# A softmax over 16 groups of 64 scores: maxima subtracted and sums taken on DVE, one wide exponential on ACT

## What is computed

```python
scores = jnp.einsum('bhqd,bhkd->bhqk', Q, K) / jnp.sqrt(jnp.float32(D))   # 16 heads, D = 32
_, topi = jax.lax.top_k(scores, k)                                        # k = min(64, S) = S
attn = jax.nn.softmax(scores * sparse_mask, axis=-1)                      # the mask is all ones
out = jnp.einsum('bhqk,bhkd->bhqd', attn, V)
```

## Time and profile before

| | before |
|---|---|
| median of three runs | 1848.55 us (1845.55 to 1848.74) |
| profiled execution | 1843.91 us, of it 1842.1 us span from first to last instruction |
| instructions | 38062 |
| mean granted TensorE clock | 0.986 |
| PE / PEld busy | 1749.4 / 1505.1 us (95% / 82% of the span) |
| DVE / ACT / POOL busy | 966.4 / 834.2 / 182.4 us (52% / 45% / 10%) |
| cross, self, ff stage | about 0 to 846.7, 846.7 to 1354.0, 1354.0 to 1842.1 us |

### The profile page before, as it was taken

The page is one execution under the profiler, slowest core; times in us unless marked ns, Lnnn a source line. Parts: engine busy times, 40 slices in busy tenths (PEclk is TensorE's granted clock), DMA queues, the critical chain, the costliest instruction groups (busy, mean ns, idle before and its releaser), DMA issues.

```text
span 1842.1 us, 38062 instructions
## 1 busy us (share of the span) xinstructions
PE 1749.4 (95%) x15364; PEld 1505.1 (82%) x15364; DVE 966.4 (52%) x1506; ACT 834.2 (45%) x2793; POOL 182.4 (10%) x267
## 2 busy tenths in 40 slices
PE   5999999999999999959999999999879999999999
PEld 4888888888888888848888888888768888888887
DVE  4655555555555555553455555555654454445433
ACT  4555555555555555546754545454432222222221
POOL 1000000000000000001121212121030111011100
PEclk9999999999999999979999999999989999999999
DMA  4011111111111111133101001010200011101000
GB/s 184 1 47 47 48 47 47 48 47 48 47 47 47 47 37 37 70 120 154 48 25 40 28 32 36 23 46 23 76 35 17 30 46 47 41 5 46 23 24 23
DMA packets 39453, 86.60 MB, mean 47 GB/s; under 512 B 4768, under 2 KB 4896, under 8 KB 38048
## 3 DMA queue, kind: packets, MB, share of 16 engines
q1 hardware_dynamic: 39328, 84.77, 12.8%
HBM read 59.58 MB, written 25.17 MB: 46 GB/s over the span
## 4 chain that ended last, share of the span: by engine, by line
PE 81%; ACT 7%; DVE 4%; POOL 3%; issue 2%; DMA 2%; SPq 0%; POOLq 0%; DVEq 0%; ACTq 0%
PE project L316 40%; PE project L1498 13%; PE scores L556 6%; ACT self_probs L368 4%; PE scores L1512 3%; PE scores L1514 3%; PE probs_t_psum L1514 3%; PE probs_t_psum L1512 3%; PE probs_t_psum L566 3%; PE attended_t L583 2%; POOL self_residual L1447 1%; DMA x<-self_residual 1%; PE probs_t_psum L1098 1%; DVE row_max L358 1%; POOL rstd L932 1%
## 5 line engine op out<-in xcount | busy, mean ns | idle before, releaser
L1498 PE MATMUL project<-ff_xt,w_ternary 128*128 128x512 f32 x1024 | 255.9, 392 | 1.7 <-DVE ff_xt L988 1.7
L1547 ACT ACTIVATE hidden<-project,b_sb 128x512 f32<-128x512 f32 x128 | 88.3, 690 | 325.3 <-PE project L1498 324.1
L1498 PEld LDWEIGHTS project<-ff_xt,w_ternary 128*128 128x128 f32 x1024 | 190.1, 188 | 40.3 <-issue 1.9
L1572 DVE CAST hidden_hi<-hidden 128x512 fp32r<-128x512 f32 x128 | 56.8, 443 | 229.8 <-ACT hidden L1547 228.9
L368 ACT ACTIVATE self_probs<-scores,exp_bias 128x64 f32<-128x64 f32 x512 | 151.9, 350 | 55.5 <-DVE exp_bias L360 55.5
L316 PE MATMUL project<-self_xt_hi,self_w_hi 128*128 128x256 f32 x512 | 149.1, 291 | 2.4 <-DVE self_xt_lo L1299 2.3
L316 PE MATMUL project<-self_xt_hi,self_w_lo 128*128 128x256 f32 x512 | 146.0, 285 | 0.7 <-ACT self_probs_t L1235 0.7
L316 PE MATMUL project<-self_xt_lo,self_w_hi 128*128 128x256 f32 x512 | 146.0, 285 | 0.0
L368 ACT ACTIVATE cross_scores_probs<-cross_scores_probs,exp_bias 128x128 f32<-128x128 f32 x256 | 99.1, 394 | 88.0 <-DVE exp_bias L360 88.0
L929 POOL TENSOR_TENSOR var_eps<-mean_var,ln_eps 128x1 f32<-128x1 f32 x96 | 19.9, 208 | 1171.1 <-DVE mean_var L793 706.2
L556 PE MATMUL scores<-cross_k_t,q_pad 128*128 128x128 f32 x1024 | 127.0, 277 | 2.8 <-DVE cross_scores L827 1.3
(11 more groups left out here) (151 smaller groups left out, 4266.0 us busy)
## 6 DMA issues: line engine op xcount, KB each, us to landing
ctx_raw<-in_ctx SPq DMA_DIRECT2D x64, 256.0 KB, 3.8
cross_x<-in_x SPq DMA_DIRECT2D x32, 256.0 KB, 2.7
x<-cross_x SPq DMA_DIRECT2D x32, 256.0 KB, 2.1
self_x<-x SPq DMA_DIRECT2D x32, 256.0 KB, 2.8
ff_w_raw<-in_w SPq DMA_DIRECT2D x2, 4096.0 KB, 18.1
x<-self_residual SPq DMA_DIRECT2D x32, 256.0 KB, 2.1
ff_x<-x SPq DMA_DIRECT2D x32, 256.0 KB, 3.6
out<-ff_residual SPq DMA_DIRECT2D x32, 256.0 KB, 2.2
```

The lines of the kernel that those rows point to most:

```text
L1498: last = nc.tensor.matmul(PJ[m % 2][:], w1_q[:, c, cols], x_t[parity(v)][:, c, :], start=(c == 0 and x_t is fxt_hi), stop=(c == DC - 1 and ...
L1547: nc.scalar.activation(h_raw[:, m % 2, :], PJ[m % 2][:], ACT.Relu, bias=b1_sb[:, m:m + 1]).then_inc(h_relu, 1)
L1572: nc.vector.tensor_copy(h_hi[:, m % 4, :], h_raw[:, m % 2, :]).then_inc(h_hi_ready, 1)
```

## The change

In the self stage alone, DVE follows its reduction of the maxima with one subtraction: it writes the scores less their group's maximum, 128x1024, from PSUM into a new SBUF tile `self_scores_shifted` (the maxima as a broadcast operand). The multiplication that made a bias goes. ACT takes one exponential of the whole 128x1024 from that tile, with the scale and no bias and no accumulator. The sums are then taken by DVE, as a reduction over the exponentials at the start of `divide`, before the reciprocal. A semaphore `s_shifted` now says that PE may write the next scores, in place of `p_ready`; `p_sum` orders the sum before the reciprocal.

```diff
--- before.py
+++ after.py
@@ -216,6 +216,7 @@
             sat_hi = sb(st, "self_at_hi", [P, DC, P], F32R)
             sat_lo = sb(st, "self_at_lo", [P, DC, P], F32R)
             f_scratch = sb(st, "ff_weight_scratch", [P, 512])
+            s_d = sb(st, "self_scores_shifted", [P, 1024])
 
             s_stages = [sq_t[:].rearrange("p a c b s -> p (a c b s)"),
                         sk_t[:].rearrange("p a c b s -> p (a c b s)"),
@@ -267,7 +268,9 @@
                 self.s_free = s("s_free")
                 self.s_max = s("s_max")
                 self.s_bias = s("s_bias")
+                self.s_shifted = s("s_shifted")
                 self.p_ready = s("p_ready")
+                self.p_sum = s("p_sum")
                 self.p_scale = s("p_scale")
                 self.p_norm = s("p_norm")
                 self.pt_full = s("pt_full")
@@ -1078,7 +1081,7 @@
 
             def scores(u, t):
 
-                wait(e, G.p_ready, total(u, NT, t))
+                wait(e, G.s_shifted, total(u, NT, t))
 
                 for c in range(DC):
                     for b in range(2):
@@ -1226,7 +1229,9 @@
                 last.then_inc(G.pj_free[bank], 1)
 
             def exponentials(u, t):
-                exponentials_of(e, G, lambda k: total(u, NT, t + k), t, HEADS, S, s_p)
+                wait(e, G.s_shifted, total(u, NT, t + 1))
+                nc.scalar.activation(s_p[:], s_d[:], ACT.Exp, scale=SCORE_SCALE) \
+                    .then_inc(G.p_ready, 1)
 
             def probs_t_out(u, t):
                 wait(e, G.pt_full, total(u, NT, t + 1))
@@ -1327,11 +1332,19 @@
                                         ALU.add).then_inc(G.pj_free[bank], 1)
 
             def maxima(u, t):
+                rows = lambda a: a[:].rearrange("p (g k) -> p g k", g=HEADS)
                 wait(e, G.s_full, total(u, NT, t + 1))
-                row_bias(e, G, lambda k: total(u, NT, t + k), t, HEADS,
-                         S[:].rearrange("p (g k) -> p g k", g=HEADS))
+                nc.vector.reduce_max(row_max[:], rows(S), AXIS.X).then_inc(G.s_max, 1)
+                wait(e, G.s_max, total(u, NT, t + 1))
+                nc.vector.tensor_tensor(rows(s_d), rows(S),
+                                        row_max[:].unsqueeze(2).to_broadcast([P, HEADS, SEQ]),
+                                        ALU.subtract).then_inc(G.s_shifted, 1)
 
             def divide(u, t):
+                wait(e, G.p_ready, total(u, NT, t + 1))
+                nc.vector.reduce_sum(row_sum[:], s_p[:].rearrange("p (g k) -> p g k", g=HEADS), AXIS.X) \
+                    .then_inc(G.p_sum, 1)
+                wait(e, G.p_sum, total(u, NT, t + 1))
                 divide_by_sums(e, G, lambda k: total(u, NT, t + k), HEADS, s_p[:])
 
             def residual(u, t, kind):
```

## The result

| | before | after |
|---|---|---|
| median | 1847.05 us (1844.70 to 1848.74) | 1826.44 us (1825.19 to 1829.39) |
| profiled execution | 1843.91, span 1842.1 | 1829.39, span 1827.6 |
| DVE busy | 966.4 | 1044.0 |
| ACT busy | 834.2 | 715.5 |

A forecast was written before the change was run, and what follows sets the result against it. PE, busy 1749.4 of 1842.1 us, was taken as the bound, stalled by ACT's queue. Terms -20.1 - 1.7 + 1.2 + 0.7 = -19.9 us took the 1848.55 us median to 1828.6; range 1819 to 1839.

The forecast's parts named there:

- PE waited for ACT's queue: Self stage, units 0 to 13: the K drain sits behind sixteen exponentials on ACT; PE waits 16.5 us in 14 pieces.
- The prices: Per tile: wide exponential 1.05 us on ACT, subtraction 1.24 and sum 1.22 on DVE; 4.63 and 0.17 removed.
- The slacks: Steady unit, tile 1: 1.0 us spare before V's first projection matmul, 1.4 before the transposes, 1.4 before V's second.
- The loop: Units 0 to 13: 14 waits gone at 1.44 us each, 20.1 gained, plus 1.7 from unit 0's softmax waits.
- The 0.26 on each wait: PE in the self stage: each wait costs 0.26 us beyond its listed length, 1.51 against 1.25.
- Unit 14: Last but one self unit: DVE divides late, after two ternary weight chunks, so the sum adds 1.2 us.
- Unit 15: Last self unit: DVE divides late, after a DMA wait; the sum adds 1.22 us, nearly paid back, net 0.7 slower.
- The 4.63 us removed from ACT: Per tile on ACT: sixteen exponentials with accumulator reads, from first start to the next instruction, 4.63 us, go away.
- (c): Rival: nothing gained, because another chain, POOL's or a DMA, sets the unit's period; 1848 us, chance 0.05.
- (d): Rival: DVE's longer path in tile 1 takes over; at three times the price 29 us slower, 1878; chance 0.03.
- (e): Rival: the wide exponential costs what the sixteen did, so ACT is not shortened; 15 us slower, 1863; chance 0.03.
- (b): Rival: part of the K drain wait stays, through dearer subtraction or exponential or late POOL; half the gain, 1839; chance 0.07.

The follow-up runs named there:

- half of the change: The changed kernel with the subtraction kept on DVE, but sixteen exponentials with accumulators on ACT and no sum on DVE: 1847.03 us, ratio 1.0005.

## Why the prediction was right

- **PE waited for ACT's queue.** Shown from both sides: taking the drain out of that queue brings each steady unit to the same 30.01 us with the old softmax (1827.25; only the 2.0 us of unit 0 are missing); a shorter queue by another way, no bias, does too (1822.11); two more exponentials bring the wait back under its name.
- **The prices.** Subtraction 1.224 us (1.24 taken), exponential 1.060 (1.05), sum 1.209 (1.22).
- **The slacks.** For the transposes of tile 1 1.54 us were there (1.4 taken), for V0 1.41 (1.0). On DVE one more sum was free and a second not, and two more exponentials on ACT were too many.
- **The loop.** Units 0 to 13 lost 3.38 + 1.36 + 1.41 + 11 x 1.49 = 22.5 us in the first pair of profiles and 23.8 in the second profile of the changed kernel; 20.1 + 1.7 = 21.8 were summed. The 0.26 on each wait was about right: 1.49 a unit for a listed 1.18, and the two added waits cost 0.21 and 0.24 us more than listed.
- **Unit 14.** The wait went from 2.39 to 3.64, 1.25 for the 1.2 forecast. The sum stands on DVE between the second chunk and the reciprocal:

```profile
1281.52 1.21 DVE L1345 TENSOR_REDUCE row_sum<-self_probs 128x16 f32<-128x1024 f32 x1
...
1283.05 1.22 DVE L383 TENSOR_TENSOR self_probs<-self_probs,row_scale 128x1024 f32<-128x1024 f32 x1
```

  The unit grew by 1.22 in one profile and by 2.39 in the other, where the lower clock lasted longer.
- **Unit 15.** The mis-sized term: 0.7 forecast, 0.9 until the transposes, and 1.73 or 4.05 for the whole unit. I had allowed 1 to 2 us for the clock; kernels with the old form differ there by 3.5 us among themselves, so most of it is the execution, not the change. I had also read the granted clock of 0.72 from a stretch that I called the end of the last unit; it is its first 30.22 us, and the unit went on to 1360.27. In the first pair of profiles the start, the clock and the tail hide about a third of the gain: 1.48 (start) - 22.5 + 2.39 + 4.05 + 0.1 = -14.5 us, where the medians say -20.6 and -22.3.
- **Luck.** The sum of -19.9 came within 1 us of the measured -20.6 partly because two misses have opposite signs: in the second profile the loop gave 2.0 us more than summed and the tail cost 2.95, not 1.9. The range would have held either alone.
- **The 4.63 us removed from ACT.** 1.48 of them were the price of the bias operand, which the prediction never named; it did not matter to its sum, since all sixteen instructions went.
- **Rivals.** (c) falls with PE busy 360.44 of 361.31 us. (d) needed 2.84 us more of DVE work on that path than the change brought; by the measured slack and gain it is 1.54 + 1.49 = 3.0, not reached by the change nor by the two spare sums. (e) falls with 1.06 us for the wide exponential. (b) did not occur, and the two more exponentials show what it would have looked like: 1834.38 us, with the wait under the name of the drain.
- **The sum.** The Trainium skill, "VectorE: DVE Perf Modes", section "Rules for kernel authors", calls `tensor_reduce` the slowest DVE op and says to consider restructuring where it is on a hot path. The trace does not show it to be slower: 1.209 us for the sum, 1.224 for the subtraction of the same size. So "the trace agrees on the price" in the prediction said too much; its own rows have 1.22 for both forms. The sum is hot in this kernel only where DVE is late, in the last two units; in the loop even a second one was free.

## What to carry to other kernels

When PE is nearly full, look for a small wait that recurs, and ask what stands ahead of the releasing instruction in its engine's queue: here a PSUM drain of 0.93 us waited behind sixteen exponentials, and moving the drain, dropping an operand or merging the exponentials each brought a steady unit to the same 30.01 us, and 19 to 25 us in all. Added work on another engine is free up to the distance, read in the timeline, between its last result and the one who takes it; look separately at the first and last iterations, where that distance is gone. And compare stretches, not whole profiles: the last unit, with the same code, took 3.5 us more in one profile than in another.

## What the runs showed of the hardware

- Small exponentials with accumulators (128x64), from start to start: 0.197 us from PSUM without a bias operand, 0.289 with one; 0.241 from SBUF without, 0.332 with. The two costs add: 0.09 us for the bias operand, 0.044 for the SBUF source. For the kernel with sixteen exponentials from SBUF I had expected them to be as long as before, so I had priced the bias at nothing on ACT, where it made 1.5 us a tile. The Trainium skill, "VectorE: DVE Perf Modes", section "The TRN2 errata — SBUF-src ops pay a fixed extra latency per instruction", gives ScalarE 224 fixed cycles from SBUF and 172 from PSUM; at the page's 1.2 GHz the difference is an estimated 0.043 us, and the trace agrees. What makes the bias cost that was not tested further than on these four forms.
- With a recurring wait of 1.2 us the granted clock stayed at 1.00 (units 3 to 13 of the kernel before); with waits of 3.1 us in each unit its mean was 0.91 and 0.95, and PE was busy 2 to 3 us longer a unit, beside the wait. The length of a wait alone does not tell: with the same 2.4 us unit 14 ran at 0.95 in the kernel before and at 1.00 in the one with half of the change.
- A wait of PE cost more than its listed length: 0.26 us more by the fixed points of the kernel before, 0.21 and 0.24 in the two kernels that added a wait.
- DVE's division took 1.22 us as a rule (median of 32; the longest 2.21) and 1.89 beside POOL's additions in tile 0 of unit 6, at no cost to PE: it had the slack there too.
